# Interleaving the two channel chunks of a scan's state tile

## The chip, the cores and the metric

The kernel runs on one core of one Trainium2 chip, as one launch. The metric is the device time of one execution in microseconds (us). The core has a matrix engine (PE, with its weight loads shown as PEld), a vector engine (DVE), a scalar engine (ACT), a general engine (POOL, also called GpSimd) and an engine that only issues transfers (SP). They run side by side and wait for each other by semaphores. On-chip memory (SBUF) has 128 partitions; the result of a matmul lands in eight banks of a second memory (PSUM), each of 128 partitions by 512 float32.

## The reference

The model has four layers over a stream of 32 sequences of 64 tokens with 256 features. Layers 0 and 2 are attention with an MLP; layers 1 and 3 are selective state space layers, each run forward and backward over the sequence and followed by a gated MLP. All is float32. What the change touches is the recurrence of layers 1 and 3, cut here to its core:

```python
def step(hst, ins):
    dt_t, B_t, C_t, x_t = ins
    dA = jnp.exp(dt_t[:, :, None] * A)
    hst = hst * dA + (dt_t * x_t)[:, :, None] * B_t[:, None, :]
    y_t = jnp.einsum('bds,bs->bd', hst, C_t)      # the factor of C, then the sum over states
    return (hst, y_t)
```

There are 512 inner channels (d) and 32 states (s) per channel in layer 1, 64 in layer 3. C depends on the token and the state, not on the channel.

## The kernel before, in words

Tokens are handled in 4 blocks of 512 (T = 512, eight sequences). A block is run in two directions, so a scan layer has RUNS = 8 runs. In a run the states are taken one after the other: `s` counts states over all runs (256 in layer 1, 512 in layer 3), and for each state the 512 channels are four chunks `j` of 128 (DC = 4), channels on the partitions and the 512 tokens along the row. One chunk of one state is one step, `q = 4 s + j`. For every state:

- ACT makes the decays, one `Exp` of 128 x 504 for each step (L1590, `decay_of`, six buffers, so up to six steps ahead), and the scaled inputs, three or four copies of 128 x 512 with B as the scale (L1609, `scale_input`, ten steps ahead).
- PE turns the scaled inputs into a PSUM bank by transposes, one bank for each step (L1057, and where only three are scaled a product with a diagonal matrix for the fourth, L1054; `scan_input`, three banks ahead).
- DVE runs the recurrence, one `tensor_tensor_scan` for each step (L2042), from the decay in SBUF and the input in PSUM into chunk `j` of a state tile. In odd runs it goes backward along the tokens.
- POOL multiplies the whole state tile in place by C (L2410): one `tensor_tensor` of 128 x 2048, where the second operand is the row of C of this state, 512 wide, repeated for the four chunks. SP brings these rows, spread over the partitions, two states at a time.
- PE transposes the products back and adds them over the states in four PSUM banks: 16 matmuls of 128 x 128 for each state (L1071, `add_up`). The state tile is the stationary operand, loaded as weights (PEld), and the identity is what streams.

The state tiles are a ring of four (`RING`), each of 2048 float32 in a partition. DVE may write a tile again once PE has added up the state four before (`sum_done`). PE's order is written out by hand: the sums of state `s` stand 9 or 10 steps behind its first scan (`Pipe.adds`), so 6 or 7 steps behind its last. Projections, norms, gates and MLP of the neighbouring blocks are the "work beside": generators that each engine takes from between its steps, by the places of a plan (`Plan`). POOL's share of these are `skip` (L2312, the row operand is one value per partition and chunk), the norm's additions and products (L2317, L2329, L2336), and `multiply`, dt times x before the next run (L2342, two ordinary row operands). POOL has one queue: what it takes from the work beside stands between two products.

The tile and its three users before:

```python
ring=[region(WORK, 11264 + 2048 * i, DC, T) for i in range(RING)]      # [partition, chunk, token]
buf["ring"][s % RING][:, j, along]                                    # DVE writes a chunk
g.tensor_tensor(state, state, c_row.unsqueeze(1).broadcast_to([P, DC, T]), ALU.mult)
buf["ring"][s % RING][:, j, t * P:(t + 1) * P]                        # PE loads 128 tokens of a chunk
```

Of the kernel before, what the change touches and what calls it, by code (L numbers as in the profile page):

```python
# [13 lines left out]
P = 128  # L14
# [4 lines left out]
T = 512  # L19
# [8 lines left out]
DC = DI // P  # L28
# [49 lines left out]
RING = 4  # L78
DECAYS = 6
# [320 lines left out]
def build(nc, a, out, c_rows):  # L400
# [4 lines left out]
    with ctx:  # L405
        def sb(name, shape, dt=f32):
            return ctx.enter_context(nc.sbuf_tensor(name, shape, dt))
# [13 lines left out]
        IDENT = sb("ident", [P, P])  # L421
# [7 lines left out]
        WC = sb("weights_c", [P, 15360])  # L429
        WORK = sb("work", [P, 21504])  # L430
        PS = ctx.enter_context(nc.psum_tensor("psum", [P, 8, T], f32))

        def region(base, at, *dims):
            n = int(np.prod(dims))
            v = base[:, at:at + n]
            if len(dims) == 1:
                return v
            names = "abcd"[:len(dims)]
            return v.rearrange(f"p ({' '.join(names)}) -> p {' '.join(names)}",
                               **{k: s for k, s in zip(names[1:], dims[1:])})  # L440
# [33 lines left out]
                    diagonal=region(WC, 14400, 2, 2, P),  # L474
                    decay=[region(WC, 11328 + 512 * i, T) for i in range(DECAYS)],
                    b=[region(WC, 14912 + 128 * i, TT, 32) for i in range(2)],
                    ring=[region(WORK, 11264 + 2048 * i, DC, T) for i in range(RING)],
                    c=region(WA, 0, 2, 2, T), xs=XS1, soft=lambda r: SOFT1)}


# [18 lines left out]
            diagonal=region(WORK, 20992, 2, 2, P),  # L499
            decay=DA3,  # L500
            b=[region(WORK, 20480 + 256 * i, TT, 64) for i in range(2)],
            ring=[region(WORK, 16384, DC, T), region(WORK, 18432, DC, T),
                  region(WC, 9728, DC, T), region(WC, 11776, DC, T)],
            c=region(WA, 0, 2, 2, T), xs=XS3, soft=lambda r: SOFT3 if r >= 0 else SOFT3A)

        most = PIPES[3].states
# [252 lines left out]
        def _(pe):  # L759

            def pipeline(l):

                pl, st, ss, buf = PIPES[l], pipe[l], scan_sems[l], AHEAD[l]
# [3 lines left out]
                def made(engine, name):  # L767
                    pe.wait_ge(st[engine].semaphore, st[engine].lead(name))
# [292 lines left out]
                def add_up(s, j):  # L1061

                    r, n = divmod(s, pl.states)
                    begins = s % (pl.states * pl.together) == 0 and j == 0
                    if begins and r >= 1:
                        made("act", f"yt@{r}")
                        made("dve", f"yt@{r}")
                    if j == 0:
                        pe.wait_ge(ss["prod_ready"], s + 1)
                    for t in range(TT):  # L1070
                        last = nc.tensor.matmul(PS[:, t, j * P:(j + 1) * P],  # L1071
                                                buf["ring"][s % RING][:, j, t * P:(t + 1) * P], IDENT[:, :],
                                                start=begins,
                                                stop=((s + 1) % (pl.states * pl.together) == 0 and j == DC - 1),
                                                is_transpose=True, skip_group_check=True)
                    if j == DC - 1:
                        last.then_inc(ss["sum_done"], 1)
# [15 lines left out]
                for q in range(-LOOKAHEAD, max(pl.adds) + 1):  # L1093
                    if q + LOOKAHEAD < pl.scans:
                        scan_input(q + LOOKAHEAD)
                    for s, j in pl.adds.get(q, ()):
                        add_up(s, j)
                    if 0 <= q < pl.scans:
                        r, step = divmod(q, pl.steps)
                        if step in SKIPS:  # L1100
                            add_skip(r, SKIPS.index(step))
                        if step == 0:
                            work = beside(r)
                            at = next(work)
                        while at is not None and (at <= step or step == pl.steps - 1):
                            at = next(work, None)
# [666 lines left out]
        def _(dve):  # L1773
            v = nc.vector
# [5 lines left out]
            def pipeline(l):  # L1780

                pl, st, ss, buf = PIPES[l], pipe[l], scan_sems[l], AHEAD[l]
# [14 lines left out]
                def zero_first(q):  # L1797

                    col = SEQ - 1 if q // pl.steps % 2 else 0
                    v.memset(by_sequence(buf["decay"][q % DECAYS])[:, :, col:col + 1], 0.0).then_inc(ss["zeroed"], 1)  # L1800
# [231 lines left out]
                for q in range(pl.scans):  # L2032
                    s, j = divmod(q, DC)
                    r, step = divmod(q, pl.steps)
                    dve.wait_ge(ss["input_ready"], q + 1)
                    dve.wait_ge(ss["decay_ready"], q + 1)
                    if j == 0 and s >= RING:
                        dve.wait_ge(ss["sum_done"], s - RING + 1)
                    if step < DECAYS:
                        dve.wait_ge(ss["zeroed"], r * DECAYS + step + 1)  # L2040
                    along = slice(None, None, -1) if r % 2 else slice(None)
                    v.tensor_tensor_scan(buf["ring"][s % RING][:, j, along], buf["decay"][q % DECAYS][:, along],  # L2042
                                         PS[:, 4 + q % LOOKAHEAD, along], 0.0, ALU.mult,
                                         ALU.add).then_inc(ss["state_ready"], 1)
                    soon = q + DECAYS - 1
                    if q > 0 and soon < pl.scans and soon % pl.steps < DECAYS:
                        dve.wait_ge(ss["state_ready"], q)
                        zero_first(soon)
                    if step == 0:
                        work = beside(r)  # L2050
                        at = next(work, None)
                    while at is not None and (at <= step or step == pl.steps - 1):
                        at = next(work, None)
# [7 lines left out]
            def attention(l, following, preceding=None):  # L2061
# [43 lines left out]
                for i in range(-1 if l == 0 else 0, NBLK + 1):  # L2105
# [160 lines left out]
                    if mlp:  # L2266
                        for c in range(KC):
                            residual("end", "down", i, c, 5 + c, vec(cfg["b2"], c), site(1))

            second, last = pipeline(1), pipeline(3)  # L2270
            attention(0, second)
            while next(second) != "tail":
# [7 lines left out]
        def _(pool):  # L2280
            g = nc.gpsimd
# [8 lines left out]
            def pipeline(l):  # L2290

                pl, st, ss, buf = PIPES[l], pipe[l], scan_sems[l], AHEAD[l]
# [112 lines left out]
                for s in range(RUNS * pl.states):  # L2405
                    if s % 2 == 0:
                        pool.wait_ge(c_loaded[l][s // 2 % 2], 16 * (s // 4 + 1))
                    pool.wait_ge(ss["state_ready"], s * DC + DC)
                    state = buf["ring"][s % RING]
                    g.tensor_tensor(state, state, buf["c"][:, s // 2 % 2, s % 2, :].unsqueeze(1).broadcast_to([P, DC, T]),  # L2410
                                    ALU.mult).then_inc(ss["prod_ready"], 1)
                    r, n = divmod(s, pl.states)
                    if n == 0:
                        work = beside(r)
                        at = next(work)
                    while at is not None and (at <= DC * (n + 1) or n == pl.states - 1):
                        at = next(work, None)
# [7 lines left out]
            def attention(l, preceding=None):  # L2425
# [6 lines left out]
                for i in range(NBLK):  # L2432
# [38 lines left out]
                    if l == 0 and i == 0:  # L2471
                        pool.wait_ge(mods_psum, SITES_AHEAD)
                        g.memset(W1["dt"][0:32, :], 0.0).then_inc(rank_zeroed, 1)

            second, last = pipeline(1), pipeline(3)
            attention(0)
            while next(second) != "tail":
# [45 lines left out]
```

## Time and profile before

| what | us |
| --- | --- |
| median of three runs | 4650.03 (4649.34 to 4650.31) |
| the profiled execution | 4648.52 |
| its span, first to last instruction | 4646.7 |
| PE busy | 4386.5 |
| DVE busy | 4144.0 |
| ACT busy | 3998.5 |
| POOL busy | 3930.1 |

Busy time is the union of an engine's instructions in the trace. A weight load (PEld) overlaps the matmul before it, and the ends of matmuls are modelled. A duration of one instruction holds its start-up and its drain; where an engine's instructions follow each other, the distance between two starts is shorter than that duration. The order in time is: attention of layer 0 up to about 328 us, the scans of layer 1 to about 1720 us, the rest of layer 1 with the attention of layer 2 to about 2058 us, the scans of layer 3 to about 4602 us, and the last block's tail.

### The profile page before, as it was taken

Reading aid. Unit: us, or ns where it says so; the run is one execution under the profiler, and the core shown is the slowest. Engines: PE = TensorE matmul, PEld = TensorE weight load, DVE = VectorE, ACT = ScalarE, POOL = GpSimd, SP = SyncE. Lnnn points to the kernel's source line nnn. Section 1 sums busy time; section 2 is a strip of 40 time slices with the busy share of each in tenths; the row PEclk is TensorE's granted clock in tenths of the full one; section 3 lists DMA queues with packets and bytes.
Section 4 is the critical chain, followed back from the end, with each engine's and each line's share of the span. In section 5 each row is a group of like instructions: output and inputs, shape, how many; then the busy total and the mean of one; then the engine's idle time right before and its main releaser. Section 6 shows DMA issues by size and latency. Waiting matters only on the chain.

```text
span 4646.7 us, 81919 instructions
## 1 busy us (share of the span) xinstructions
PE 4386.5 (94%) x32260; PEld 3640.8 (78%) x32260; DVE 4144.0 (89%) x4037; ACT 3998.5 (86%) x6263; POOL 3930.1 (85%) x1047
## 2 busy tenths in 40 slices
PE   8989899899899998999999999999999999999998
PEld 4448788788788884458888888888888888888887
DVE  6669999999999986759999999999998999999996
ACT  3459799799889974559999999999999999999995
POOL 4429899889889985539999999999998999999996
PEclk8999999999999999999999999999999999999999
DMA  4001111111111221022242232322321322323221
GB/s 162 1 17 66 58 57 64 54 57 63 56 56 58 67 78 39 1 39 69 74 84 73 88 64 72 84 68 78 84 70 66 84 78 76 76 74 64 76 77 41
DMA packets 241391, 303.40 MB, mean 65 GB/s; under 512 B 116448, under 2 KB 175712, under 8 KB 241008
## 3 DMA queue, kind: packets, MB, share of 16 engines
q1 hardware_dynamic: 241008, 298.15, 22.2%
q8 instruction: 257, 4.21, 0.4%
q14 instruction: 126, 1.03, 0.1%
HBM read 289.84 MB, written 8.26 MB: 64 GB/s over the span
## 4 chain that ended last, share of the span: by engine, by line
PE 45%; ACT 32%; DVE 13%; issue 6%; POOL 4%; DVEq 0%; DMA 0%; SPq 0%; POOLq 0%; ACTq 0%
PE psum L1071 11%; PE psum L1057 9%; PE psum L799 8%; ACT work L1590 8%; ACT work L1609 7%; ACT weights_c L1590 7%; DVE work L2042 6%; PE psum L1054 5%; PE psum L1171 5%; ACT weights_c L1609 4%; DVE weights_c L2042 3%; POOL work L2410 3%; ACT L1372 2%; PE psum L1247 2%; DVE work L1879 1%
## 5 line engine op out<-in xcount | busy, mean ns | idle before, releaser
L2410 POOL TENSOR_TENSOR work<-work,weights_a 128x2048 f32<-128x2048 f32 x512 | 2332.0, 4576 | 242.0 <-DVE work L2042 240.2
L2042 DVE TENSOR_TENSOR_SCAN work<-weights_c,psum 128x512 f32<-128x512 f32 x1366 | 1569.8, 1201 | 93.9 <-PE psum L1057 80.4
L1071 PE MATMUL psum<-ident,work 128*128 128x128 f32 x8192 | 1238.2, 275 | 15.7 <-ACT weights_a L1398 8.1
L2410 POOL TENSOR_TENSOR weights_c<-weights_c,weights_a 128x2048 f32<-128x2048 f32 x256 | 1168.6, 4582 | 57.9 <-DVE weights_c L2042 57.4
L1590 ACT ACTIVATE work<-work,decay 128x504 f32<-128x504 f32 x1366 | 968.3, 709 | 45.8 <-DVE work L2042 22.7
L1071 PEld LDWEIGHTS psum<-ident,work 128*128 128x128 f32 x8192 | 969.0, 142 | 19.9 <-POOL work L2410 10.4
L1057 PE MATMUL psum<-ident,work 128*128 128x128 f32 x5464 | 943.9, 275 | 41.3 <-ACT weights_c L1609 30.4
L2042 DVE TENSOR_TENSOR_SCAN weights_c<-work,psum 128x512 f32<-128x512 f32 x684 | 789.7, 1200 | 30.1 <-PE psum L1057 29.3
L2042 DVE TENSOR_TENSOR_SCAN work<-work,psum 128x512 f32<-128x512 f32 x682 | 786.6, 1199 | 30.7 <-PE psum L1057 18.9
L1057 PEld LDWEIGHTS psum<-ident,work 128*128 128x128 f32 x5464 | 667.9, 142 | 140.5 <-issue 67.3
L1057 PE MATMUL psum<-ident,weights_c 128*128 128x128 f32 x4432 | 771.2, 275 | 0.0
L1071 PE MATMUL psum<-ident,weights_c 128*128 128x128 f32 x4096 | 621.1, 275 | 6.6 <-POOL weights_c L2410 6.4
L1057 PEld LDWEIGHTS psum<-ident,weights_c 128*128 128x128 f32 x4432 | 548.7, 143 | 0.0
L1590 ACT ACTIVATE weights_c<-work,decay 128x504 f32<-128x504 f32 x682 | 484.1, 710 | 35.3 <-DVE weights_c L2042 17.3
L1609 ACT ACTIVATE work<-work 128x512 f32<-128x512 f32 x683 | 487.5, 714 | 13.5 <-PE psum L1247 13.5
L1071 PEld LDWEIGHTS psum<-ident,weights_c 128*128 128x128 f32 x4096 | 485.5, 143 | 9.7 <-POOL weights_c L2410 9.3
L1609 ACT ACTIVATE work<-weights_a,work 128x512 f32<-128x512 f32 x683 | 486.4, 712 | 0.0
L1590 ACT ACTIVATE weights_c<-weights_a,weights_c 128x504 f32<-128x504 f32 x512 | 360.2, 709 | 95.9 <-DVE work L2042 93.8
L2042 DVE TENSOR_TENSOR_SCAN weights_c<-weights_c,psum 128x512 f32<-128x512 f32 x340 | 396.6, 1200 | 14.2 <-PE psum L1057 12.1
L1590 ACT ACTIVATE weights_c<-work,weights_c 128x504 f32<-128x504 f32 x512 | 356.6, 707 | 25.0 <-DVE work L2042 24.6
L1054 PEld LDWEIGHTS psum<-work 128*128 128x128 f32 x1368 | 219.8, 192 | 113.6 <-issue 72.8
L1054 PE MATMUL psum<-work,weights_a 128*128 128x128 f32 x1368 | 284.3, 290 | 19.2 <-DVE weights_c L2042 8.8
(192 smaller groups left out, 5785.1 us busy)
## 6 DMA issues: line engine op xcount, KB each, us to landing
weights_a<-c_rows SPq DMA_DIRECT2D x384, 512.0 KB, 3.6
work<-b_diagonals SPq DMA_DIRECT2D x240, 128.0 KB, 2.2
weights_c<-b_diagonals SPq DMA_DIRECT2D x112, 128.0 KB, 2.1
b_diagonals<-weights_c SPq DMA_DIRECT2D x1, 4096.0 KB, 16.3
weights_c<-in_L_cond_fwd_in_w SPq DMA_DIRECT2D x8, 512.0 KB, 5.4
weights_c<-in_L_cond_fwd_xproj_w SPq DMA_DIRECT2D x4, 1024.0 KB, 7.0
weights_c<-in_L_cond_bwd_in_w SPq DMA_DIRECT2D x8, 512.0 KB, 5.3
weights_c<-in_L_cond_bwd_xproj_w SPq DMA_DIRECT2D x4, 1024.0 KB, 7.2
```

The costliest lines, as they stand in the source:

```text
L799: last = nc.tensor.matmul(PS[0:rows, bank, :], weights[k], moving[k], start=(k == 0), stop=(k == len(moving) - 1))
L1054: nc.tensor.matmul(PS[:, bank, SCALED * P:T], buf["dtx"][r % 2][:, SCALED, j * P:(j + 1) * P], buf["diagonal"][:, s // 2 % 2, s % 2, :], s ...
L1057: last = nc.tensor.transpose(PS[:, bank, t * P:(t + 1) * P], buf["scaled"][s % INPUTS][t][:, j * P:(j + 1) * P], IDENT[:, :])
L1071: last = nc.tensor.matmul(PS[:, t, j * P:(j + 1) * P], buf["ring"][s % RING][:, j, t * P:(t + 1) * P], IDENT[:, :], start=begins, stop=((s ...
L1171: last = nc.tensor.matmul(PS[:, bank, :], weights[k], moving[k], start=(k == 0), stop=(k == len(moving) - 1))
L1247: last = nc.tensor.matmul(PS[:, 5 + c, :], W2A[:, k, c * P:(c + 1) * P], G[l][:, k, :], start=(k == 0), stop=(k == MLP // P - 1))
L1372: act.add_instruction(mybir.InstLoadActFuncSet(name=nc.get_next_instruction_name(), engine=act.engine, act_func_set_id=which, ins=[], outs ...
L1590: f(seqs[:, :, lo:lo + SEQ - 1], dts[:, :, lo:lo + SEQ - 1], ACT.Exp, scale=rate).then_inc(ss["decay_ready"], 1)
L1609: last = f(buf["scaled"][s % INPUTS][t], buf["dtx"][r % 2][:, t, :], ACT.Copy, scale=weight)
L1879: v.scalar_tensor_tensor(out=to[:, :, inside], in0=of, scalar=weight, in1=plus[:, :, inside], op0=ALU.mult, op1=ALU.add).then_inc(done(f"c ...
L2042: v.tensor_tensor_scan(buf["ring"][s % RING][:, j, along], buf["decay"][q % DECAYS][:, along], PS[:, 4 + q % LOOKAHEAD, along], 0.0, ALU.mult,
L2410: g.tensor_tensor(state, state, buf["c"][:, s // 2 % 2, s % 2, :].unsqueeze(1).broadcast_to([P, DC, T]), ALU.mult).then_inc(ss["prod_ready ...
```

## The change

The state tile keeps its 2048 elements in a partition, in another order: [2, T, 2] in place of [4, T]. Chunk `j` lies at pair `j // 2`, token `t`, place `j % 2`, so its address is 1024 (j // 2) + 2 t + j % 2. The elements of one chunk are two elements (8 bytes) apart. DVE writes with that step, PE loads its stationary operand with that step, and the product reads and writes the tile from its first to its last element as before, while its C operand is read as c0, c0, c1, c1 and so on, 512 pairs, twice over. Nothing is added or taken away: no instruction, no semaphore, no transfer, no buffer.

```diff
@@ AHEAD[1]
-                    ring=[region(WORK, 11264 + 2048 * i, DC, T) for i in range(RING)],
+                    ring=[region(WORK, 11264 + 2048 * i, 2, T, 2) for i in range(RING)],
@@ AHEAD[3]
-            ring=[region(WORK, 16384, DC, T), region(WORK, 18432, DC, T),
-                  region(WC, 9728, DC, T), region(WC, 11776, DC, T)],
+            ring=[region(WORK, 16384, 2, T, 2), region(WORK, 18432, 2, T, 2),
+                  region(WC, 9728, 2, T, 2), region(WC, 11776, 2, T, 2)],
@@ add_up (PE)
-                                                buf["ring"][s % RING][:, j, t * P:(t + 1) * P], IDENT[:, :],
+                                                buf["ring"][s % RING][:, j // 2, t * P:(t + 1) * P, j % 2], IDENT[:, :],
@@ the scan (DVE)
-                    v.tensor_tensor_scan(buf["ring"][s % RING][:, j, along], buf["decay"][q % DECAYS][:, along],
+                    v.tensor_tensor_scan(buf["ring"][s % RING][:, j // 2, along, j % 2], buf["decay"][q % DECAYS][:, along],
@@ the product (POOL)
-                    g.tensor_tensor(state, state, buf["c"][:, s // 2 % 2, s % 2, :].unsqueeze(1).broadcast_to([P, DC, T]),
+                    row = buf["c"][:, s // 2 % 2, s % 2, :]
+                    g.tensor_tensor(state, state, row.unsqueeze(1).unsqueeze(3).broadcast_to([P, 2, T, 2]),
                                     ALU.mult).then_inc(ss["prod_ready"], 1)
```

## Rows read from the trace of the kernel before

**Rows 1.** The page: shares of the span on the chain, by line.

```profile
PE psum L1071 11%; PE psum L1057 9%; PE psum L799 8%; ACT work L1590 8%; ACT work L1609 7%; ACT weights_c L1590 7%; DVE work L2042 6%; PE psum L1054 5%; PE psum L1171 5%; ACT weights_c L1609 4%; DVE weights_c L2042 3%; POOL work L2410 3%; ACT L1372 2%; PE psum L1247 2%; DVE work L1879 1%
```

**Rows 2.** Stretch, length; busy PE, PEld, DVE, ACT, POOL (instructions); granted clock, DMA, GB/s.

```profile
328.00:1720.00 1392.00, 1310.00 (x9935) 1147.21 (x9933) 1299.84 (x1285) 1255.01 (x1964) 1244.08 (x299) 0.98 0.19 60
2058.00:4602.00 2544.00, 2436.62 (x18922) 2156.56 (x18923) 2436.34 (x2299) 2450.36 (x3901) 2424.18 (x566) 0.99 0.27 74
```

**Rows 3.** Timeline (start us, us): products back to back, four scans.

```profile
2959.80 9.11 POOL L2410 TENSOR_TENSOR work<-work,weights_a 128x2048 f32<-128x2048 f32 x2
2968.87 9.10 POOL L2410 TENSOR_TENSOR weights_c<-weights_c,weights_a 128x2048 f32<-128x2048 f32 x2
...
2995.95 4.53 DVE L2042 TENSOR_TENSOR_SCAN work<-work,psum 128x512 f32<-128x512 f32 x4
```

**Rows 4.** Products and other POOL operations, by form (busy us, mean ns; idle before).

```profile
L2410 POOL TENSOR_TENSOR work<-work,weights_a 128x2048 f32<-128x2048 f32 x512 | 2332.0, 4576 | 242.0 <-DVE work L2042 240.2
L2342 POOL TENSOR_TENSOR weights_a<-work 128x1024 f32<-128x1024 f32 x14 | 33.5, 2391 | 0.0
L2312 POOL TENSOR_TENSOR work<-work,vectors 128x1024 f32<-128x1024 f32 x32 | 61.3, 1917 | 0.0
L2392 POOL TENSOR_TENSOR weights_a<-work,modulation 128x512 f32<-128x512 f32 x2 | 2.1, 1042 | 1.3 <-DVE work L2017 1.3
```

**Rows 5.** PE waits on POOL in layer 1's scans (total us, times, longest).

```profile
PE psum L810 <- POOL work L2342: 10.3, 3, 6.8
PE psum L799 <- POOL normed L2336: 3.9, 3, 2.6
```

**Rows 6.** Timeline of POOL before two of these waits end.

```profile
503.17 4.59 POOL L2410 TENSOR_TENSOR work<-work,weights_a 128x2048 f32<-128x2048 f32 x1
507.69 1.93 POOL L2329 TENSOR_TENSOR scratch<-scratch,modulation 128x1024 f32<-128x1024 f32 x1
509.55 13.66 POOL L2410 TENSOR_TENSOR work<-work,weights_a 128x2048 f32<-128x2048 f32 x3
523.14 1.92 POOL L2336 TENSOR_TENSOR normed<-scratch,modulation 128x1024 f32<-128x1024 f32 x1
...
619.14 9.09 POOL L2410 TENSOR_TENSOR work<-work,weights_a 128x2048 f32<-128x2048 f32 x2 [0.56 <-DVE work L2042]
628.20 2.38 POOL L2342 TENSOR_TENSOR work<-work 128x1024 f32<-128x1024 f32 x1
630.55 4.52 POOL L2410 TENSOR_TENSOR work<-work,weights_a 128x2048 f32<-128x2048 f32 x1
635.04 2.34 POOL L2342 TENSOR_TENSOR work<-work 128x1024 f32<-128x1024 f32 x1
```

**Rows 7.** Chain at the ends of the two scan stretches (start us, us, what).

```profile
1716.65 9.08 POOL work L2410 x2
...
4582.71 6.79 POOL work L2410 x2
...
4591.74 9.00 POOL weights_c L2410 x2
```

**Rows 8.** PE waits on POOL's product, 2060 to 4605 us.

```profile
PE psum L1071 <- POOL weights_c L2410: 6.4, 7, 2.5
PE psum L1071 <- POOL work L2410: 2.4, 5, 0.7
```

**Rows 9.** By form: the scan, weight loads of sums and diagonals, a copy.

```profile
L2042 DVE TENSOR_TENSOR_SCAN work<-weights_c,psum 128x512 f32<-128x512 f32 x1366 | 1569.8, 1201 | 93.9 <-PE psum L1057 80.4 <-ACT weights_c L1590 10.6 <-PE psum L1071 0.6
L1930 DVE COPY work<-psum 128x512 f32<-128x512 f32 x64 | 42.8, 669 | 2.5 <-PE psum L799 2.5
L1071 PEld LDWEIGHTS psum<-ident,work 128*128 128x128 f32 x8192 | 969.0, 142 | 19.9 <-POOL work L2410 10.4 <-ACT weights_a L1398 9.2
L1054 PEld LDWEIGHTS psum<-work 128*128 128x128 f32 x1368 | 219.8, 192 | 113.6 <-issue 72.8 <-DVE weights_c L2042 12.0 <-ACT work L1609 10.4
```

## The prediction

> **What bounds the kernel now.** I read the busy times by stretch first. The two scan stretches are 1392 and 2544 us of the 4646.7 us span [rows 2], and every changed instruction lies in them. In layer 3's stretch PE, DVE, ACT and POOL are busy for 2437, 2436, 2450 and 2424 us of 2544: four engines within 1.1% of each other, POOL with 120 us to spare. In layer 1's they have 1310, 1300, 1255 and 1244 of 1392, POOL 148 us to spare. So no single engine is the bound; one that gets faster gives up only the waits of others that it ends, one that gets slower uses up its own spare time and then sets the pace.
>
> The timeline says how near they are state by state. Two products start 2968.87 - 2959.80 = 9.07 us after the two before, 4.54 us for each. Four scans in a row last 4.53 us; their own duration is about 1.20 us [rows 9], so (4.53 - 1.20) / 3 = 1.11 us from start to start and 4.44 us a state [rows 3]. POOL is thus a touch slower than DVE wherever DVE has no other work, and catches up while DVE does other work.
>
> Then the chain of waits: the products are 3% of it, some 139 us, while PE's transposes (L1071, L1057) and ACT's copies and decays have 46% [rows 1]. Its POOL pieces lie in layer 1 and at the two ends [rows 7]; read window by window, layer 3's stretch from 2060 to 4580 us shows none among its costliest lines. So the product, the largest single group of the page (768 of them), is mostly off the path. That is the first thing to see: a large saving in it is worth little.
>
> **The product.** No instruction is added or removed; what can change is the duration of three kinds. The product's tile is still read and written from first to last; only C is read in pairs of one address. The trace has both neighbours of that pattern. With two ordinary rows: (4576 - 2391) / 1024 = 2.134 ns an element [rows 4]. With one operand that stays at one address (L2312 for 512 elements at a time, L2392 for 64): (1917 - 1042) / 512 = 1.709 ns [rows 4]. So POOL does save when the second address doesn't move: 0.425 ns an element. A product of 2048 at the lower rate would take 1917 + 1024 x 1.709 = 3667 ns, 909 ns less. That is one end. The other end: pairs may be read as rows of two elements, each with a start of its own, for which the trace has no row; I bound the loss by the same 909 ns with the other sign (5485 ns), since it is the only difference between access patterns that the trace prices. Between them: what is saved follows how often the address moves; in an ordinary row it moves at every element, here at every second, so half the saving, 455 ns, product 4121 ns. I take this value. It is an estimate from [rows 4], not a measurement.
>
> What of it lies on the path: 768 x 0.455 = 349 us of POOL's busy time become idle. The time gained is place by place:
>
> - PE waits for POOL before the transposes L810 three times, 10.3 us in all, longest 6.8; for the norm's result (L799) three times, 3.9 us, longest 2.6 [rows 5]. POOL is late there because products stand ahead of the wanted operation in its queue. Before the 6.8 us wait POOL last waited at 619.14, and three products run until L2342 ends [rows 6]: 3 x 0.455 = 1.4 us. The two other L810 waits have two products each: 0.9 us each, 3.2 us together. Before the 2.6 us wait the queue is full for at least five products (four of them in [rows 6]): 2.3 us; the two other L799 waits (1.3 us together) go entirely. Sum 3.2 + 2.3 + 1.3 = 6.8 us. What is late next at these places is the operation itself (L2342, 2.3 to 2.4 us, not changed) and ACT.
> - At the end of each scan stretch nothing covers the last products: two on the chain in layer 1 (9.08 us), and 6.79 + 9.00 us in layer 3 with scans between them [rows 7]. 2 x 0.455 = 0.9; of the 3.5 products in layer 3 I count the last two wholly and half of the others, 2.7 x 0.455 = 1.2. Sum 2.1 us.
> - In layer 3 PE waits for the product 12 times, 8.8 us [rows 8], at places that aren't on the chain, so PE's lost time there is made up beside ACT's and DVE's work. Between 0 and 8.8; I take 1.
>
> Sum 6.8 + 2.1 + 1 = 9.9, so 10 us. Check against the chain: its 139 us of products shortened by 10% are 14 us, which nothing of this kind can exceed while the chain stays. The likeliest case's own range is thus 2 to 16 us. The cover of POOL's remaining saving is ACT, DVE and PE at 96% of layer 3 [rows 2].
>
> The Trainium skill has a rule against this: its GPSIMD Engine Reference, section Instruction dispatch, says that the two reads of a two-input operation share one port, so that some 2.5 cycles an element are a floor of such an operation. By it pairs would save nothing and the kernel would stay where it is. The trace agrees for two ordinary rows and not for a resting operand; whether pairs belong to the one or the other it doesn't show.
>
> **The scan's write.** 3072 scans write with a step of 8 bytes. No write with a step stands in the rows. A scan takes 1201 ns for 512 elements, 2.3 ns each; a DVE copy of 512 takes 669 ns, 1.3 ns each [rows 9]. So the scan's writes come at little over half the rate at which DVE can write, and I take 0. The upper end is a write at half the copy's rate: 2 x 669 = 1338, +137 ns for each scan. Nothing makes a step faster than no step, so the lower end is 0.
>
> **PE's weight load.** 12288 loads of the sums read their 128 elements with that step. Again no row has it; the load takes 142 ns, and its slower neighbour of the same size, the diagonal product's, 192 ns [rows 9]. The two ends are 0 (a gain has no cause, the elements read are as many) and +50 ns. I take 0: the diagonal product's operand is also read without a step, so its 192 ns isn't a price of the step. This is the least supported choice here. The Trainium skill, SBUF — State Buffer, gives lines of 16 bytes that want two hits each, which a step of 8 bytes still has; no run here shows it.
>
> **Sum.** The profiled execution takes 4648.52 us, 1.8 outside its span. 4648.5 - 10 = 4638.5. The median of the runs is 1.5 above the profiled execution, so 4640 us.
>
> **Rivals.**
>
> 1. *The pairs save nothing* (the product stays at 4576 ns). For it: a saving is seen only where the address rests for 64 elements or more. Time 4650, give or take 2.
> 2. *The whole saving* (3667 ns), if only the innermost step counts. At the L810 waits 2.7 + 1.8 + 1.8, at L799 all 3.9, at the ends 2 x 0.909 and 2.7 x 0.909, together 4.3, in layer 3 half of 8.8: 18.9 us, and by the chain at most 28. Time 4631.
> 3. *Pairs cost POOL time*, the other side. Place: POOL's queue in both scan stretches. It decides from the point where POOL's spare time is used up: 120 / 512 = 0.23 us a state in layer 3, a product above 4.81 us; 148 / 256 = 0.58 us in layer 1. At 5485 ns it costs 512 x 0.909 - 120 = 345 and 256 x 0.909 - 148 = 85: time 5080. For it: 1024 rows of two elements are a pattern that no row of the trace has. Against it: rows of 64 (L2392) give with rows of 512 (L2312) a start-up of 1042 - 512 x 1.709 = 167 ns, no more than the 206 ns of two ordinary rows (4576 - 2048 x 2.134), so a row's start costs nothing that can be seen.
> 4. *PE's load slows*: 12288 x 50 ns = 614 us less PE's spare 82 + 107 = 189 us [rows 2]: +425, time 5075; it decides from 107 us / 8192 = 13 ns a load in layer 3.
> 5. *DVE's write slows*: 3072 x 137 ns = 421 less DVE's spare 92 + 108 = 200: +221, time 4871.
>
> **How the numbers follow.** The forecast 0.38; rival 1 0.29; rival 2 0.10; rival 3 0.12; rival 4 0.08; rival 5 0.03. A measurement of this kernel tells about 0.2%, 9.3 us, from no change. Of the forecast's 0.38 some 0.23 gain more than that, and all of rival 2: faster 0.33. Rival 1 and the rest of the forecast: same 0.44. Rivals 3 to 5: slower 0.23. The range goes down to 4622, the chain's limit for rival 2 (0.03 below it), and up to 4700, which takes in mild forms of rivals 3 to 5 (a product of 4.9 us costs 512 x 0.32 - 120 = 46 us) and leaves 0.17 above.
>
> **What would show it.** The product's mean (L2410): 4121 by the forecast, 4576 by rival 1, 3667 by rival 2, above 4810 for slower. The scan at 1200 and the load L1071 at 142 if both steps are free. POOL busy in layer 3 down by 512 x 0.455 = 233 us with PE, DVE and ACT busy unchanged, its idle time waiting for DVE's scans; the L810 and L799 waits on POOL down to about 7 and 0.3 us. The forecast is wrong if the mean of any of the three instructions moves the other way, or if the product falls and the time moves by more than 16 us: then POOL was on the path in layer 3 and the chain hid it.

## The result, and the profile after

The changed kernel takes 4682.12 us (median; 4679.6 to 4685.22) beside 4650.17 us (4649.34 to 4651.71) of the kernel before on the same chip: ratio 1.007, 95% interval 1.0055 to 1.0085. It is slower by 32 us; the forecast was 4640. Its profiled execution took 4685.22 us with a span of 4683.4.

The page of the changed kernel, first the busy times, then the chain of waits by engine and by line. In the kernel before, the chain was 45% PE, 32% ACT, 13% DVE and 4% POOL.

```profile
PE 4463.5 (95%) x32260; PEld 3784.7 (81%) x32260; DVE 4153.5 (89%) x4037; ACT 4004.9 (86%) x6263; POOL 3596.9 (77%) x1047
...
PE 59%; ACT 25%; DVE 10%; issue 4%; POOL 2%; DVEq 0%; DMA 0%; SPq 0%; POOLq 0%; ACTq 0%
PE psum L1071 18%; PE psum L1057 13%; PE psum L799 11%; PE psum L1054 7%; ACT work L1590 6%; ACT work L1609 6%; ACT weights_c L1590 5%; PE psum L1171 5%; DVE work L2042 4%; ACT weights_c L1609 3%; DVE weights_c L2042 2%; ACT L1372 2%; PE psum L1247 1%; DVE work L1879 1%; POOL work L2411 1%
```

PE's sums (L1071) went from 11% of the chain [rows 1] to 18%, and the product (now L2411) from 3% to 1%. The chain moved onto PE. The same kernel by form shows the three kinds of instruction that the change touches, and the matmuls that go with the changed loads (busy us, mean ns, idle before and its releaser):

```profile
L2411 POOL TENSOR_TENSOR work<-work,weights_a 128x2048 f32<-128x2048 f32 x512 | 2104.8, 4114 | 489.4 <-DVE work L2042 488.3 <-DMA weights_a<-c_rows 0.5
L2042 DVE TENSOR_TENSOR_SCAN work<-weights_c,psum 128x512 f32<-128x512 f32 x1366 | 1571.1, 1201 | 102.7 <-PE psum L1057 87.5 <-ACT weights_c L1590 11.7 <-PE psum L1071 1.2
L1071 PE MATMUL psum<-ident,work 128*128 128x128 f32 x8192 | 1317.8, 284 | 10.1 <-ACT weights_a L1398 8.0 <-POOL work L2411 2.2
L1071 PEld LDWEIGHTS psum<-ident,work 128*128 128x128 f32 x8192 | 1142.3, 205 | 11.5 <-ACT weights_a L1398 9.1 <-POOL work L2411 2.4
L1071 PE MATMUL psum<-ident,weights_c 128*128 128x128 f32 x4096 | 656.5, 283 | 2.2 <-POOL weights_c L2411 2.2
```

The same two forms of PE in the kernel before:

```profile
L1071 PE MATMUL psum<-ident,work 128*128 128x128 f32 x8192 | 1238.2, 275 | 15.7 <-ACT weights_a L1398 8.1 <-POOL work L2410 7.5
L1071 PE MATMUL psum<-ident,weights_c 128*128 128x128 f32 x4096 | 621.1, 275 | 6.6 <-POOL weights_c L2410 6.4
```

Product 4576 to 4114 ns [rows 4], scan 1201 as before, weight load 142 to 205 ns [rows 9]. The load overlaps the matmul ahead of it, so PE doesn't lose those 63 ns: its busy time per matmul rises from (1238.2 + 621.1) / 12288 = 151.3 ns to (1317.8 + 656.5) / 12288 = 160.7, some 9.4. The timeline says the same: four sums in a row of one state (start us, length, what), kernel after, then kernel before; the other groups of four in the stretches read (about 45 in each of three stretches of 60 us) have the same two lengths.

```profile
3021.97 0.64 PE L1071 MATMUL psum<-ident,weights_c 128*128 128x128 f32 x4
```

```profile
3009.05 0.60 PE L1071 MATMUL psum<-ident,work 128*128 128x128 f32 x4
```

From start to start that is (0.64 - 0.284) / 3 = 0.119 us after and (0.60 - 0.275) / 3 = 0.108 before: some 10 ns more for each of the 12288, by a length given to 0.01 us.

The two stretches of [rows 2], same bounds, in the kernel after, and then PE's waits on POOL in layer 1's scans (total us, times, longest) beside [rows 5]:

```profile
328.00:1720.00 1392.00, 1327.32 (x9860) 1188.27 (x9861) 1292.77 (x1277) 1253.81 (x1963) 1125.52 (x297) 0.98 0.19 60
2058.00:4602.00 2544.00, 2460.21 (x18676) 2221.79 (x18675) 2415.51 (x2275) 2429.51 (x3859) 2169.89 (x559) 0.99 0.28 74
```

```profile
PE psum L810 <- POOL work L2342: 7.2, 3, 5.8
PE psum L799 <- POOL normed L2336: 0.4, 1, 0.4
```

In layer 3's window PE does 246 matmuls fewer than before (18676 to 18922) and is busy for 24 us more, at the same granted clock, 0.99. The other engines do less in it, since the work has slid past its end: from the first scan to the last, layer 3 takes 2563.7 us instead of 2533.0 and layer 1 takes 1398.5 instead of 1390.0. POOL's waits did shrink as forecast (10.3 to 7.2 and 3.9 to 0.4 us), so it looks as if the expected gain came and a larger loss covers it; the first two experiments below show both apart.

### The profile page after: what moved, and what is told of

It is laid out like the page before. It is cut to its first block, busy times and chain, and to the rows that moved or that the text cites. A ratio compares the mean times of both kernels' runs of the same rounds, so it can differ in the third digit from the quotient of the medians.

```text
span 4683.4 us, 81919 instructions
## 1 busy us (share of the span) xinstructions
PE 4463.5 (95%) x32260; PEld 3784.7 (81%) x32260; DVE 4153.5 (89%) x4037; ACT 4004.9 (86%) x6263; POOL 3596.9 (77%) x1047
## 4 chain that ended last, share of the span: by engine, by line
PE 59%; ACT 25%; DVE 10%; issue 4%; POOL 2%; DVEq 0%; DMA 0%; SPq 0%; POOLq 0%; ACTq 0%
PE psum L1071 18%; PE psum L1057 13%; PE psum L799 11%; PE psum L1054 7%; ACT work L1590 6%; ACT work L1609 6%; ACT weights_c L1590 5%; PE psum L1171 5%; DVE work L2042 4%; ACT weights_c L1609 3%; DVE weights_c L2042 2%; ACT L1372 2%; PE psum L1247 1%; DVE work L1879 1%; POOL work L2411 1%
## 5 line engine op out<-in xcount | busy, mean ns | idle before, releaser
L2411 POOL TENSOR_TENSOR work<-work,weights_a 128x2048 f32<-128x2048 f32 x512 | 2104.8, 4114 | 489.4 <-DVE work L2042 488.3
L2042 DVE TENSOR_TENSOR_SCAN work<-weights_c,psum 128x512 f32<-128x512 f32 x1366 | 1571.1, 1201 | 102.7 <-PE psum L1057 87.5
L1071 PE MATMUL psum<-ident,work 128*128 128x128 f32 x8192 | 1317.8, 284 | 10.1 <-ACT weights_a L1398 8.0
L2411 POOL TENSOR_TENSOR weights_c<-weights_c,weights_a 128x2048 f32<-128x2048 f32 x256 | 1053.0, 4116 | 178.5 <-DVE weights_c L2042 178.2
L1071 PEld LDWEIGHTS psum<-ident,work 128*128 128x128 f32 x8192 | 1142.3, 205 | 11.5 <-ACT weights_a L1398 9.1
L1057 PE MATMUL psum<-ident,work 128*128 128x128 f32 x5464 | 942.5, 275 | 36.1 <-ACT weights_c L1609 29.1
L1057 PEld LDWEIGHTS psum<-ident,work 128*128 128x128 f32 x5464 | 672.1, 143 | 123.7 <-issue 64.4
L1057 PE MATMUL psum<-ident,weights_c 128*128 128x128 f32 x4432 | 771.5, 275 | 0.0
L1071 PE MATMUL psum<-ident,weights_c 128*128 128x128 f32 x4096 | 656.5, 283 | 2.2 <-POOL weights_c L2411 2.2
L1071 PEld LDWEIGHTS psum<-ident,weights_c 128*128 128x128 f32 x4096 | 569.2, 205 | 2.5 <-POOL weights_c L2411 2.4
L1057 PEld LDWEIGHTS psum<-ident,weights_c 128*128 128x128 f32 x4432 | 548.0, 143 | 0.0
L1054 PE MATMUL psum<-work 128*128 128x128 f32 x1368 | 275.2, 283 | 19.8 <-ACT work L1609 8.2
```

Source lines behind the costliest of these rows:

```text
L1054: nc.tensor.matmul(PS[:, bank, SCALED * P:T], buf["dtx"][r % 2][:, SCALED, j * P:(j + 1) * P], buf["diagonal"][:, s // 2 % 2, s % 2, :], s ...
L1057: last = nc.tensor.transpose(PS[:, bank, t * P:(t + 1) * P], buf["scaled"][s % INPUTS][t][:, j * P:(j + 1) * P], IDENT[:, :])
L1071: last = nc.tensor.matmul(PS[:, t, j * P:(j + 1) * P], buf["ring"][s % RING][:, j // 2, t * P:(t + 1) * P, j % 2], IDENT[:, :], start=begi ...
L2042: v.tensor_tensor_scan(buf["ring"][s % RING][:, j // 2, along, j % 2], buf["decay"][q % DECAYS][:, along], PS[:, 4 + q % LOOKAHEAD, along] ...
L2411: g.tensor_tensor(state, state, row.unsqueeze(1).unsqueeze(3).broadcast_to([P, 2, T, 2]), ALU.mult).then_inc(ss["prod_ready"], 1)
```

## The experiments

### The three parts alone

All three leave the tile as it was and change one reader or writer only, so they handle other elements than the reference wants.

`e1_pe_only`, the weight load alone:

```diff
-    buf["ring"][s % RING][:, j, t * P:(t + 1) * P], IDENT[:, :],
+    buf["ring"][s % RING].rearrange("p c t -> p (c t)").rearrange("p (a t c) -> p a t c", t=T, c=2)[:, j // 2, t * P:(t + 1) * P, j % 2], IDENT[:, :],
```

> The kernel before, with PE's weight loads of the sums alone reading with the step of 8 bytes (the elements are another chunk's, so the sums are of other numbers; the work is the same). DVE and POOL as before. Theory A, the stepped weight load is the whole loss and POOL's product a small gain: load L1071 205 ns as in the changed kernel, product 4576 ns, time 4650 + 32 + 10 = 4692 us (4680 to 4710), slower than the changed kernel. Theory B, the loss comes from POOL's or DVE's part and the longer load is hidden under the matmul before: load 205 ns, time 4650.

Measured: 4697.06 us (4695.89 to 4698.09) beside 4649.9; ratio 1.0099, interval 1.0083 to 1.0114. By form, chain by engine, and layer 3's window, set as in [rows 2] from 1.7 us before its first scan to 9.3 us after the start of its last:

```profile
L1071 PE MATMUL psum<-ident,work 128*128 128x128 f32 x8192 | 1319.1, 284 | 15.0 <-POOL work L2410 7.6 <-ACT weights_a L1398 7.0
L1071 PEld LDWEIGHTS psum<-ident,work 128*128 128x128 f32 x8192 | 1142.5, 205 | 19.6 <-POOL work L2410 11.4 <-ACT weights_a L1398 8.2
```

```profile
PE 57%; ACT 25%; DVE 9%; POOL 6%; issue 4%; DMA 0%; DVEq 0%; SPq 0%; POOLq 0%; ACTq 0%
```

```profile
2072.50:4650.40 2577.90, 2490.64 (x18920) 2251.39 (x18921) 2444.96 (x2299) 2456.22 (x3901) 2428.22 (x566) 0.99 0.27 73
```

The load's step alone costs 47 us, more than the whole change does, with POOL's product untouched. The window holds the same work as the one of before (18920 matmuls to 18922); it is 34 us longer, PE is busy in it for 54 us more, and idle for 2577.9 - 2490.6 = 87 us, where it was 107. So PE's spare time was not used up first: of the 54 us, 20 went into it while the time grew by 34.

`e2_pool_only`, the product alone, C in pairs over the plain tile:

```diff
-    g.tensor_tensor(state, state, buf["c"][:, s // 2 % 2, s % 2, :].unsqueeze(1).broadcast_to([P, DC, T]),
+    tile = buf["ring"][s % RING].rearrange("p c t -> p (c t)").rearrange("p (a t c) -> p a t c", t=T, c=2)
+    row = buf["c"][:, s // 2 % 2, s % 2, :]
+    g.tensor_tensor(tile, tile, row.unsqueeze(1).unsqueeze(3).broadcast_to([P, 2, T, 2]),
```

> The kernel before, with C alone read in pairs (the tile keeps its order, so the products are with other factors of C; the work is the same). Theory A and my forecast's sum: product 4114 ns, load 142 ns, time 4640 us (4634 to 4648). Rival, a faster product is wholly hidden: 4650. Theory B, the product's new pattern or its place in time disturbs others: above 4655.

Measured: 4636.6 us (4634.12 to 4637.28); ratio 0.9968, interval 0.9956 to 0.9981. By form, and PE's waits on POOL in layer 1:

```profile
L2411 POOL TENSOR_TENSOR work<-work,weights_a 128x2048 f32<-128x2048 f32 x512 | 2099.8, 4106 | 460.4 <-DVE work L2042 460.2
```

```profile
PE psum L810 <- POOL work L2342: 7.7, 3, 5.8
PE psum L799 <- POOL normed L2336: 1.0, 3, 0.7
```

Thirteen us faster, where the forecast's ten came from the same step. Layer 1's scans are 6.0 us shorter (1384.0), layer 3's not at all (2532.8 to 2533.0); 3.9 us come between the layers and 2.5 at the end; what shortens these two, beyond the last products of each stretch with 0.47 us less each, was not looked into. (The profiled executions differ by 11.2 us, since the first scan starts 1.4 us later in this one.)

`e3_dve_only`, the scan's write with a step of 8 bytes:

```diff
-    v.tensor_tensor_scan(buf["ring"][s % RING][:, j, along], ...
+    v.tensor_tensor_scan(buf["ring"][s % RING].rearrange("p c t -> p (c t)").rearrange("p (a t c) -> p a t c", t=T, c=2)[:, j // 2, along, j % 2], ...
```

> The kernel before, with DVE's scans alone writing with the step of 8 bytes (other order of the tile, so other values in the sums; same work). Theory A: the scan stays at 1200 ns and the time at 4650 us (within 4). Rival, the stepped write costs where POOL works beside it: product or scan longer, time above 4660.

Measured: 4650.19 us (4648.9 to 4652.34); ratio 1.0, interval 0.9991 to 1.0009; the scan stays at 1200 ns. The step of a scan's write is free. The three add up: -13.3 + 47.2 + 0.3 = +34, and the change measured +32.

### How the load's price depends on the step and on the number of loads

`e5_pe_step4`: as `e1_pe_only` with a step of four elements (16 bytes).

```diff
+    buf["ring"][s % RING].rearrange("p c t -> p (c t)").rearrange("p (t c) -> p t c", c=4)[:, t * P:(t + 1) * P, j], IDENT[:, :],
```

> As e1_pe_only, but the weight loads of the sums read with a step of four elements, 16 bytes (other elements, same work). Theory A1, the load pays for each line of memory that it touches, so the price grows with the step: load well above e1's 205 ns (about 142 + 3 x 63 = 331 if each further element of step costs the same), time above 4850 us. Theory A2, any step costs the same: load 205 ns and 4697 us as in e1.

Measured: 4702.39 us (4700.55 to 4704.47); ratio 1.0113, interval 1.0099 to 1.0126.

```profile
L1071 PEld LDWEIGHTS psum<-ident,work 128*128 128x128 f32 x8192 | 1159.2, 209 | 18.4 <-POOL work L2410 10.2 <-ACT weights_a L1398 8.1
```

Side by side 142 ns, every second element 205, every fourth 209: nearly the whole price is for having a step at all, little of it for its size. The time is 53 us above the kernel before, 5 more than in `e1_pe_only`.

`e9_pe_half`: as `e1_pe_only`, but only every second chunk's loads (6144) have the step.

```diff
+    (buf["ring"][s % RING]...[:, j // 2, t * P:(t + 1) * P, j % 2] if j % 2 else
+     buf["ring"][s % RING][:, j, t * P:(t + 1) * P]), IDENT[:, :],
```

> As e1_pe_only, but only every second chunk's loads (6144 of 12288) have the step of 8 bytes. Theory A3, PE's spare time is used up first, as rival 4 of my forecast reckons it: the first half of the added PE time (about 60 us of 119) is mostly swallowed, the loss is under 12 us: below 4662. Theory A4, PE is on the path in part of the time everywhere, so each stepped load costs its share at once: half of e1's 47 us, 4673 us (4668 to 4679).

Measured: 4672.4 us (4664.01 to 4677.09); ratio 1.0047, interval 1.0034 to 1.0059.

```profile
L1071 PE MATMUL psum<-ident,work 128*128 128x128 f32 x8192 | 1276.9, 279 | 15.3 <-ACT weights_a L1399 7.9 <-POOL work L2411 7.2
L1071 PEld LDWEIGHTS psum<-ident,work 128*128 128x128 f32 x8192 | 1054.3, 174 | 19.7 <-POOL work L2411 10.3 <-ACT weights_a L1399 9.0
```

Layer 3's window, set as before:

```profile
2068.20:4630.30 2562.10, 2465.76 (x18926) 2209.28 (x18927) 2440.74 (x2299) 2454.36 (x3901) 2425.55 (x566) 0.99 0.28 74
```

Half of the loads cost 22.5 us (by the interval 16 to 27), half of 47.2 within what the runs, 13 us apart, can tell. A cushion used up first would have made this half cheap or free. The window agrees: PE is busy for 29 us more than before and the window is 18 us longer, 0.62 of it; in `e1_pe_only` it was 34 of 54, 0.63. Fewer loads than half were not tried.

### Interleaved tiles without a stepped load

`e4_flat2`: the whole change, but PE loads 128 elements that lie side by side (64 tokens of two chunks). Its sums then come out in woven order; x is kept woven too, so that the skip term fits, and the rare gate product on DVE reads PSUM with a step. Its core against the changed kernel:

```diff
-    buf["ring"][s % RING][:, j // 2, t * P:(t + 1) * P, j % 2], IDENT[:, :],
+    buf["ring"][s % RING].rearrange("p a t c -> p (a t c)")[:, j * T + t * P:j * T + (t + 1) * P], IDENT[:, :],
...
+    XS1 = XS3 = region(WORK, 3072, 2, T, 2)
```

> A full kernel: the tile in pairs as in the changed kernel, but PE loads 128 elements that lie side by side (64 tokens of two chunks), and the order is undone later: x is kept in the same order, and DVE's gate product after the sums (L1825) reads PSUM in steps. So POOL's and DVE's new patterns stay and the stepped weight load of the sums goes; a few per run of others become stepped (20 moving operands of 512, 4 gate products). Theory A: load 142 ns, product 4114 ns, time 4640 us (4632 to 4650). Theory B: as slow as the changed kernel, 4682.

Measured: 4643.68 us (4640.49 to 4646.21); ratio 0.9985, interval 0.9976 to 0.9994. By form, this kernel and then the kernel before:

```profile
L1076 PEld LDWEIGHTS psum<-ident,work 128*128 128x128 f32 x8192 | 971.0, 143 | 12.4 <-ACT weights_a L1404 9.4 <-POOL work L2421 3.0
L806 PE MATMUL psum<-work,weights_c 128*80 128x512 f32 x64 | 32.9, 614 | 6.4 <-ACT work L1457 6.4
```

```profile
L799 PE MATMUL psum<-work,weights_c 128*80 128x512 f32 x64 | 31.5, 595 | 4.9 <-ACT work L1451 4.9
```

The load is back at 143 ns and the loss is gone; the cause is shown from both sides. What keeps it 7 us behind `e2_pool_only` lies in layer 3: its scans take 2539.8 us to 2532.8 there, layer 1's 1384.2 to 1384.0. What the rows show is the woven x as a moving operand of PE: 614 instead of 595 ns, here and in the 452 matmuls of 128*128 (613 to 595; 234.4 to 226.0 us busy). In layer 3's window PE is busy for 9 us more than in `e2_pool_only` (2446.4 to 2437.2); at the 0.63 of `e1_pe_only` that would be 6 of the 7 us, an estimate. No run tests it alone.

`e6_flat4`: the same with all four chunks interleaved, x included, so the steps that remain are 16 bytes.

```diff
-    XS1 = XS3 = region(WORK, 3072, 2, T, 2)
+    XS1 = XS3 = region(WORK, 3072, 1, T, 4)
...
-    ring=[region(WORK, 11264 + 2048 * i, 2, T, 2) for i in range(RING)],
+    ring=[region(WORK, 11264 + 2048 * i, 1, T, 4) for i in range(RING)],
```

> As e4_flat2 with all four chunks interleaved (C read as four times the same address), loads of the sums side by side, x in the same order, so with a step of 16 bytes for the scans' writes, for the 20 moving operands of a run and for the skip's and multiply's operands on POOL. By the rule that POOL saves for each repeated address: product 4576 - 0.75 x 909 = 3894 ns. Theory A: PE's stepped moving operands cost e4's 7 us or some more, POOL's further saving brings 3 to 6 us: 4640 us (4630 to 4660). Rival, a step of 16 bytes is dear wherever it stands: scan above 1250 ns or stepped matmuls above 700 ns, time above 4680.

Measured: 4857.55 us (4856.6 to 4857.76); ratio 1.0446, interval 1.0431 to 1.046. By form:

```profile
L2421 POOL TENSOR_TENSOR work<-work,weights_a 128x2048 f32<-128x2048 f32 x512 | 1979.3, 3870 | 692.1 <-DVE work L2052 686.3 <-DMA weights_a<-c_rows 5.8
L2322 POOL TENSOR_TENSOR work<-work,vectors 128x1024 f32<-128x1024 f32 x32 | 78.5, 2455 | 0.0
L806 PE MATMUL psum<-work,weights_c 128*80 128x512 f32 x64 | 61.8, 1077 | 18.2 <-ACT work L1457 18.2
L1939 DVE COPY work<-psum 128x512 f32<-128x512 f32 x64 | 57.4, 897 | 1.7 <-PE psum L806 1.7
```

The group of 64 copies mixes 32 of the gate's input, which stay side by side, with 32 of x, which are stepped. DVE's timeline keeps them apart (start us, length; an x copy, then one without a step):

```profile
2204.32 1.12 DVE L1939 COPY work<-psum 128x512 f32<-128x512 f32 x1
2547.62 0.67 DVE L1939 COPY work<-psum 128x512 f32<-128x512 f32 x1
```

This is a miss: 4640 was expected. Of the rival's two signs one came (stepped matmuls above 700 ns) and one didn't (the scan stays at 1203 to 1204). The product falls to 3870 ns, but x in steps of 16 bytes is dear: PE's moving operand 1077 ns (595), DVE's copy into it 1.06 to 1.18 us (0.67), POOL's operation with a resting operand 2455 (1917 [rows 4]). Against `e4_flat2` PE is busy for 199 us more (4594.9 to 4396.1), DVE for 45, and the time is 214 us longer. A saving on POOL, which is mostly off the path, was bought with time on PE and DVE, which are on it.

### The skip term moved off PE

`e7_skip2`: as `e4_flat2`, but x stays plain, and POOL adds the skip term to one chunk of four states' products in each run, instead of PE's 256 transposes.

```diff
+    if n in SKIPS[l]:
+        j = SKIPS[l].index(n)
...
+        part = state[:, j // 2, :, j % 2]
+        last = g.tensor_tensor(part, part, XS1[:, j, :], ALU.add)
```

> As e4_flat2, but x keeps its plain order; the skip term D x is added by POOL to one chunk of four states' products in each run (four additions of 128 x 512), where PE had 16 transposes a run. Theory A: without stepped moving operands the 7 us that e4 lacks come back, and PE loses 256 transposes of 0.12 us (31 us of its busy time, a third to two thirds of it on the path); POOL has the time: 4625 us (4612 to 4638). Rival, POOL is late after the additions and PE waits for the products of the first states of each run (waits L1076 on POOL above 20 us): 4640 or more.

Measured: 4661.45 us (4658.96 to 4664.98); ratio 1.0025, interval 1.0016 to 1.0035: a miss. Waits in layer 1's scans (total us, times, longest):

```profile
ACT L1366 <- POOL work L2418: 19.3, 4, 5.0
PE psum L806 <- POOL normed L2334: 9.9, 3, 4.7
PE psum L817 <- POOL work L2340: 7.7, 3, 5.9
```

Layer 3's scans are 3.4 us shorter than in the kernel before, layer 1's are 21 us longer. In layer 1 ACT waits for the addition four times (L2418, 19.3 us; no such wait before), since this kernel lets it write the next x only after the fourth one, and PE waits 9.9 us for the norm's result, 3.9 before [rows 5], behind the additions in POOL's queue. The rival expected PE to wait for the products themselves instead, above 20 us; those waits are 9.4 us in the whole run. That the waits named make up the 21 us is my reading.

`e8_skip4`: as `e7_skip2` with tiles of four, where POOL has 240 ns a product more to spare.

> As e7_skip2 with all four chunks interleaved, so that C is read four times from one address. Theory A: product 3894 ns, scan 1200 ns, and 1 to 4 us less than e7_skip2. Rival, the scan's write with a step of 16 bytes slows (above 1250 ns): 3072 x 50 ns = 150 us more.

Measured: 4656.95 us (4650.25 to 4660.22); ratio 1.0014, interval 1.0005 to 1.0022. Product 3869 ns, scan 1203, additions 1570 to 1589 ns instead of 1304 to 1308. Layer 1's cost stays in large part: its scans are 14 us longer than in the kernel before, by the profiled execution.

`e10_mixed2`: layer 1 as in `e4_flat2`, layer 3 as in `e7_skip2`, each where it had done well.

```diff
-    XS1 = XS3 = region(WORK, 3072, 2, T, 2)
+    XS1, XS3 = region(WORK, 3072, 2, T, 2), region(WORK, 3072, DC, T)
...
+    if l == 3 and n in ADDED:
```

> A full kernel from the parts that paid: tiles in pairs, PE's loads side by side; in layer 1 x in pairs and the skip term by PE (as e4_flat2), in layer 3 x plain and the skip term added by POOL (as e7_skip2). By the stretches of e4_flat2 (layer 1 ends as early as in e2) and e7_skip2 (layer 3's scans 10 us shorter than e4's): 4643.7 - 10 = 4634 us (4628 to 4640), faster than the kernel before by 0.3%. Rival, layer 3 of e7_skip2 was short only because it began otherwise: 4640 or more.

Measured: 4637.18 us (4636.46 to 4638.64) beside 4649.89; ratio 0.9973, interval 0.9963 to 0.9984: faster than both kernels, by 0.27% than before and, across the runs, by 45 us than the changed one. By form, and the chain by engine:

```profile
L2423 POOL TENSOR_TENSOR work<-work,weights_a 128x2048 f32<-128x2048 f32 x512 | 2101.3, 4109 | 442.9 <-DVE work L2053 436.0 <-DMA weights_a<-c_rows 6.6
L1077 PEld LDWEIGHTS psum<-ident,work 128*128 128x128 f32 x8192 | 968.6, 142 | 12.2 <-ACT weights_a L1405 9.2 <-POOL work L2423 3.0
```

```profile
PE 45%; ACT 32%; DVE 14%; issue 6%; POOL 2%; DVEq 0%; DMA 0%; SPq 0%; POOLq 0%; ACTq 0%
```

The chain is that of the kernel before, with POOL's 4% halved. Layer 3's scans take 2531.4 us, where `e4_flat2` has 2539.8; the rival falls. It is as fast as `e2_pool_only`, with the whole computation in it, and 3 us slower than the 4634 expected.

`e11_mixed4`: the same with layer 3's tiles in fours, 240 ns less a product in that layer (its scans then take 2531.5 us).

> As e10_mixed2 with layer 3's tiles in fours (product 3870 ns there, as in e6 and e8). Theory A, POOL isn't on layer 3's path any more after pairs: within 2 us of e10_mixed2. Rival, POOL's additions for the skip still make PE wait and shorter products help: 4 us or more faster.

Measured: 4637.6 us (4635.61 to 4639.23); ratio 0.9974, interval 0.9964 to 0.9984. Equal to `e10_mixed2`: in layer 3 a faster product is worth nothing any more, as `e2_pool_only` had shown.

## Why the prediction was wrong

The step that failed is "PE's weight load": "I take 0". The load takes 205 ns, and that step alone costs 47 us (`e1_pe_only`). The text called it the least supported choice and gave rival 4, with this very mechanism, 0.08. The argument for 0 was that the elements read are as many as before; `e1_pe_only` and `e5_pe_step4` show that not their number but their not lying side by side is paid for. The measured +63 ns lies outside the ends 0 and +50: the upper one was a neighbour's duration, which had nothing to do with a step.

Rival 4 had the mechanism and a price nine times too high: +425 us, measured +47. Both halves of its formula failed, in opposite directions.

- It charged the load's duration, 12288 x 50 ns. Loads run beside the matmul ahead of them; what PE pays is the time from one matmul to the next, 10 ns for 63 ns of load. By L1071's rows that is (1319.1 + 661.4) - (1238.2 + 621.1) = 121 us; the page's whole PE busy time rises less, from 4386.5 to 4465.4 us in `e1_pe_only`, 79 us.
- It subtracted PE's spare time, 189 us. With the right price of 121 us that rule gives no loss at all, and with half the loads too; measured are 47 and 22.5. That PE's 107 idle us of layer 3 lie at places where it isn't on the chain, and so don't cover the places where it is, is my reading; what is shown is that half the loads cost half. Of PE's added busy time by the page, 0.52 to 0.60 came out as time: 22.5 of 43.5 us in `e9_pe_half`, 47.2 of 78.9 in `e1_pe_only`, 52.7 of 94.6 in `e5_pe_step4`. PE's share of the chain before, 45%, is thus too low a factor in all three, and in `e6_flat4` by far (214 us longer than `e4_flat2` for 199 us of PE, with DVE's 45 beside them). Only with the 121 us of L1071's rows does it come near (0.45 x 121 = 54; 0.45 x 57.8 = 26 for half the loads), and there it is too high. No share was tested by a forecast made before the run.

The forecast had a sum of this kind as an upper limit of the product's gain: 139 us of the chain shortened by 10% are 14, and 13.3 were measured. One such agreement doesn't make it a rule: layer 3's products became shorter by the same 10%, and its scans by 0.2 us.

Point by point, the rest held:

- The product: forecast 4121 ns, measured 4106 to 4114. The guess that the saving follows how often C's address moves also gives 4576 - 909 x 3/4 = 3894 for fours; measured 3870. Rivals 1 to 3 fall.
- The gain: forecast 10 us, `e2_pool_only` 13. L810's waits fell by 2.6 (forecast 3.2), L799's by 2.9 (3.6); layer 3 gave 0 (1 forecast). Mis-sized was what lies outside the two stretches: 2.5 us at the tail and 3.9 between the layers, for which the forecast had 2.1, the ends of both stretches.
- The last sign of being wrong: "if the product falls and the time moves by more than 16 us", POOL was on the path in layer 3. Both happened, and the conclusion is false: with the product alone (`e2_pool_only`) layer 3's scans stay at 2532.8 us. The sign looked for one cause where three changes were made at once. The sign that held is the other one, the mean of the load moving.
- The scan's write: 0, as forecast (`e3_dve_only`); rival 5 falls.

The range reached up to 4700 for "mild forms" of the dear rivals and so held 4682, which is luck: that part of it was worked out for a product of 4.9 us, and the product became faster. The chance of slower, 0.23, was low for three access patterns of which no row of the trace had one.

## What to carry to other kernels

Price a slower instruction by what it adds to the time from one start to the next on its engine, not by its duration, and don't subtract the engine's idle time first when several engines are busy for 96% of a stretch. Here half to six tenths of what PE was busy longer came out as time, where the additions were small and spread over every state. When a layout makes one engine faster, count the instructions whose reads or writes become stepped: here the engine with 4% of the chain gained and the one with 45% paid. The step can be moved to a rarer operation: reading the tile flat and unweaving the result turned +32 us into -6, and with x left plain and the skip term moved off PE in layer 3 into -13.

## What the runs showed of the hardware

- POOL's product of 2048 elements takes 4576 ns with two moving addresses, 4106 to 4114 with the second in pairs and 3870 in fours; its rate is no fixed figure for two operands. The saving is 0.51 and 0.78 of the 909 ns that the forecast took as the whole, near the half and three quarters of a rule by which only a moving address costs; the rule has these two points and no more.
- PE's load of 128x128 in f32 takes 142 ns side by side, 205 with a step of 8 bytes and 209 with 16. 63 ns more of load move the start-to-start time of 128-column matmuls by 10 ns. PE's moving operand of 512 is another matter: 595, 614 and 1077 ns.
- A scan's write has a free step, 1200 to 1204 ns at 4, 8 and 16 bytes, while a copy of 512 takes 0.67 us side by side and into steps of 8 bytes, and 1.06 to 1.18 us into steps of 16. That is still less than the scan's 1.20, which fits the reading that an operation slow by itself hides the step; no run tests it. POOL's operation of 1024 with a resting operand takes 1917 ns side by side, 1914 with x in steps of 8 bytes and 2455 in steps of 16.
